# Cutting the side-row loads and running-row stores of two gather passes into fifths, one behind each group of steps

## What is computed

```
x = layernorm(x + EdgeConv(x, src, dst))            # max over a node's edges of MLP([x_i, x_j - x_i])
x = layernorm(x + NodeUpdate(x, mean of edge_attr))  # mean over the edges that leave a node
x = layernorm(x + Mean(x, src, dst))                 # msg = segment_sum(x[src], dst) / degree, gate, linear
x = layernorm(x + Attention(x, src, dst, types))     # segment softmax over dst of 4 heads, typed weights
```

## Time and profile before

| | |
|---|---|
| runs (us) | 19606.31, 19635.21, 19637.1; median 19635.21 |
| the profiled execution: its time, its span | 19425.3 us, 19423.5 us |
| POOL busy in the span | 13120.1 us, 68% |
| DVE busy | 7110.8 us, 37% |
| PE busy | 4712.7 us, 24% |
| SP's DMA queue (q1) | 1,029,704 packets, 830.45 MB, 14.2% of 16 DMA engines' span |
| POOL's DMA queue (q0) | 416,960 packets, 533.81 MB, 12.1% |

### The profile page before, as it was taken

The page is one execution under the profiler, slowest core; times in us unless marked ns, Lnnn a source line. Parts: engine busy times, 40 slices in busy tenths (PEclk is TensorE's granted clock), DMA queues, the critical chain, the costliest instruction groups (busy, mean ns, idle before and its releaser), DMA issues.

```text
span 19423.5 us, 125968 instructions
## 1 busy us (share of the span) xinstructions
PE 4712.7 (24%) x20806; PEld 3710.9 (19%) x20806; DVE 7110.8 (37%) x16320; ACT 1013.1 (5%) x4397; POOL 13120.1 (68%) x13050
## 2 busy tenths in 40 slices
PE   3221221221666666666510000000032000000002
PEld 2100010000566665566410000000021000000001
DVE  5444444443333433333331111111123444444444
ACT  0000000000000000000000000000022000000000
POOL 4666666667666666666657777777755666666665
PEclk9655555555555555555555555555566555555555
DMA  2222222221333333333211121211123333333332
GB/s 71 76 70 68 69 69 67 66 70 51 93 93 91 91 92 93 92 93 93 71 41 45 47 47 47 47 47 47 45 84 121 97 97 97 95 95 97 97 95 55
DMA packets 1464730, 1467.46 MB, mean 76 GB/s; under 512 B 727134, under 2 KB 1226293, under 8 KB 1464536
## 3 DMA queue, kind: packets, MB, share of 16 engines
q1 hardware_dynamic: 1029704, 830.45, 14.2%
q0 software_dynamic: 416960, 533.81, 12.1%
q10 hardware_dynamic: 18000, 102.41, 1.3%
HBM read 863.04 MB, written 602.69 MB: 75 GB/s over the span
## 4 chain that ended last, share of the span: by engine, by line
issue 31%; another core or an unknown queue 19%; DVE 18%; POOL 17%; PE 10%; DVEq 2%; DMA 2%; ACT 1%; SPq 0%; POOLq 0%; ACTq 0%
POOL gat L643 16%; PE pair L1011 4%; DVE oh_lo L1294 2%; DVE prod L1306 2%; DVE oh_hi L1296 2%; PE bank L1000 2%; DVE cur L1391 1%; DVE run_sb L1661 1%; DMA gat<-tab_t,gi 1%; DVE ar L1684 1%; DVE ag_idx L1310 1%; PE bank L1002 1%; PE bank L988 1%; DVE run_sb L1693 1%
## 5 line engine op out<-in xcount | busy, mean ns | idle before, releaser
L600 POOL DMA_INDIRECT perm<-at,ag_idx x3125 | 3135.3, 1003 | 1575.6 <-issue 937.5
L643 POOL DMA_INDIRECT gat<-tab_b,gi x3125 | 3121.2, 999 | 1588.0 <-issue 968.1
L643 POOL DMA_INDIRECT gat<-tab_x,gi x3125 | 3307.4, 1058 | 1191.1 <-issue 1187.7
L643 POOL DMA_INDIRECT gat<-tab_t,gi x3125 | 3027.8, 969 | 1373.5 <-issue 902.5
L1032 PE MATMUL pair<-ident,tails 128*64 128x128 f32 (+1 forms) x20 | 4.9, 421 | 8795.8 <-DVE tails L1474 4423.6
L1011 PE MATMUL pair<-blk,ohb 128*128 128x65 f32 x7500 | 1765.3, 422 | 12.5 <-DVE ohb L1416 12.3
L1032 PEld LDWEIGHTS pair<-ident,tails 128*64 128x64 f32 (+1 forms) x20 | 3.1, 170 | 8797.5 <-DVE tails L1474 4424.4
L1584 DVE TENSOR_TENSOR run_sb<-p,gat 128x320 f32<-128x320 f32 x625 | 314.9, 504 | 3702.2 <-DMA gat<-tab_x,gi 3691.9
L1011 PEld LDWEIGHTS pair<-blk,ohb 128*128 128x128 f32 x7500 | 1645.8, 329 | 88.0 <-DVE ohb L1416 14.0
L961 PE MATMUL bank<-oh_s,lo_bf 128*128 128x490 bf16 x625 | 368.2, 589 | 3219.1 <-DVE prod L1306 2638.4
L1290 DVE TENSOR_TENSOR oh_s<-iota_bf,st_sh 128x490 bf16<-128x490 bf16 x625 | 417.6, 668 | 1760.3 <-remote 1431.9
(11 more groups left out here) (283 smaller groups left out, 9830.6 us busy)
## 6 DMA issues: line engine op xcount, KB each, us to landing
edge<-start_rows SPq DMA_DIRECT2D x250, 800.0 KB
run<-run_sb SPq DMA_DIRECT2D x250, 800.0 KB
blk<-perm SPq DMA_DIRECT2D x750, 165.0 KB
run<-run_sb SPq DMA_DIRECT2D x125, 900.0 KB
at<-in_edge_attr SPq DMA_DIRECT2D x625, 160.0 KB
start_rows<-zeros ACTq DMA_DIRECT2D x125, 800.0 KB
tab_t<-trow SPq DMA_DIRECT2D x98, 512.0 KB
perm<-at,ag_idx POOLq DMA_INDIRECT x3125
```

Of the source, the lines that this page charges most:

```text
L600: pool.indirect_dma_start(perm_d, rows(perm_d, ag_idx[tp][:, k, s:s + 1]), at[tp][:, s, k, :], None).then_inc(a_sc[tp], 16)
L643: pool.indirect_dma_start(gat[:, k, s, 0:width], None, table, rows(table, gi[tp][:, s, k:k + 1])).then_inc(g_in[k], 16)
```

## The change

In passes c and d, SP issues each tile's store, and in pass d each tile's load, as five DMAs, one for each chain index s (a fifth: 128 pieces, one per partition; 160 KB, and 180 KB for the store of pass d). Fifth s waits for `t * KS + min(s, 3)` instead of `t * KS`, so the fifths come one behind each step of the tile, and the last two behind the same one. Loads and stores alternate. Pass b keeps its whole transfers. The waits of DVE at L1576, L1665 and L1666, of SP at the pass's end and of POOL before the node stages (L650) count five DMAs per tile in place of one. Nothing else changes.

```diff
             def edge_io(c, side_done, run_done, run_d, width, with_side):
+                in_fifths = c != "b"
...
+                def load_fifth(t, tp, s):
+                    sp.dma_start(edge0[tp][:, s].rearrange("p k f -> p (k f)"),
+                                 chains(starts_d)[:, s, bass.ds(t * (KS * F), KS * F)]).then_inc(e_in[tp], 16)
+
+                def store_fifth(t, tp, s):
+                    sp.dma_start(chains(run_d)[:, s, bass.ds(t * (KS * width), KS * width)],
+                                 run_view(tp, width)[:, s].rearrange("p k f -> p (k f)")).then_inc(r_out[tp], 16)
 
                 def body(t, tp):
...
-                    if with_side:
+                    if not in_fifths:
                         sp.wait_ge(side_done, t * KS)
                         load(t + 1, 1 - tp)
-                    sp.wait_ge(run_done, t * KS)
-                    store(t - 1, 1 - tp)
-
-                if with_side:
+                        sp.wait_ge(run_done, t * KS)
+                        store(t - 1, 1 - tp)
+                        return
+                    for s in range(SUB):
+                        step = min(s, KS - 2)
+                        if with_side:
+                            sp.wait_ge(side_done, t * KS + step)
+                            load_fifth(t + 1, 1 - tp, s)
+                        sp.wait_ge(run_done, t * KS + step)
+                        store_fifth(t - 1, 1 - tp, s)
...
+                if with_side and in_fifths:
+                    for tp in range(2):
+                        for s in range(SUB):
+                            load_fifth(tp, tp, s)
...
             def phase_d(t, tp, first):
                 v.wait_ge(d_st, t * 2 + 2)
-                v.wait_ge(e_in[tp], sides(1, t, tp))
-                v.wait_ge(r_out[tp], sides(2, t, tp))
+                v.wait_ge(e_in[tp], sides_d(t, tp))
+                v.wait_ge(r_out[tp], stored_by_fifths(2, t, tp))
```

34 lines of the change are left out of this document (24 added, 10 removed).

## The result

| | kernel before | changed kernel |
|---|---|---|
| runs | 13 | 13 |
| median (us) | 19615.96 | 19675.53 |
| lowest to highest (us) | 19592.66 to 19639.93 | 19635.13 to 19707.54 |
| ratio of the times | 1 | 1.0027, 95% interval 1.002 to 1.0034 |

What follows compares the result with a forecast made beforehand. POOL was taken to bound the kernel, busy 68% of the span. Terms -130 - 75 - 50 + 8 = -247 us took the profiled 19425.3 to 19178, or 19388 us for the runs' median; 8-in-10 range 18990 to 19720.

Steps and rivals of the forecast that it cites:

- The floor of 1.247 us a gather: POOL in passes c and d: 3125 gathers need 3897 us, leaving 459 and 504 us that smoother transfers could give back.
- The store in pass c, -130 us: Pass c: a whole store costs POOL 1.94 us, five fifths 0.85; 1.1 us gained in 118 tiles, 130 us.
- The price of a fifth, 0.85 us from pass b: Pass c: a tile's five fifths cost POOL 5 x 0.17 = 0.85 us, half of what pass b's block loads showed.
- The wait before the second step of pass d, -75 us: Pass d: the whole load delays gathers, so POOL waits 0.84 us; fifths save 0.6 us in 125 tiles, 75 us.
- The eighth of DVE's slow stretches, -50 us: Pass d: fewer slow DVE stretches coincide with late gathers, saving an eighth of the remaining 429 us, 50 us.
- SyncE's cost, taken as 0 with bounds 0 and 138 us: Pass d: SP issues ten DMAs a tile; DVE might wait 1.1 us for the last store, but 0 was taken.
- The ends, +8 us: Outside the loops of passes c and d: fifths add four issues of 0.64 us at three places, 8 us.
- Rival 1: Passes c and d: transfers were hidden anyway and stalls only move to other gathers; about 19606 us, chance 0.19.
- Rival 3: Pass d: SP falls behind issuing ten DMAs, so DVE waits for its last store; +250 us, 19885 us, chance 0.17.
- Rival 2: Passes c and d: transfer bursts make the slow stretches, so most surplus goes; 720 us less, 18915 us, chance 0.14.

Runs made afterwards that it cites:

- e2: Kernel before with stores in fifths in pass c only, pass d whole; 19593.07 us, ratio 0.9999.
- e5: Kernel before with each gather of pass c bringing rows to 64 partitions instead of 128; 19448.33 us, ratio 1.0003.
- e6: Kernel before with the stores of pass c holding 16 of 128 partitions; 19451.24 us, ratio 1.0005.
- e9: Kernel before with POOL gathering four of the five groups of a step in pass c; 18705.62 us, ratio 0.9536.
- e12: Kernel before with pass d's loads and stores moving 32 of 128 partitions, in whole transfers; 1.440 us a gather in the pass's middle.
- e3: Kernel before with loads and stores in fifths in pass d only, pass c whole; 19645.11 us, ratio 1.0029.
- e10: Kernel before with pass d's loads and stores in fifths, all ten behind a tile's first step; 19668.39 us, ratio 1.0027.
- e11: Kernel before with whole transfers and eight added one-row stores a tile in pass d; 19691.35 us, ratio 1.0036.
- e13: Kernel before with 24 more SyncE waits a tile in pass d (empty instructions absorbed), no further transfer; 19500.65 us, ratio 1.0037.
- e17: The changed kernel again, unaltered, on a chip without pauses; 16949.56 us, ratio 0.9974 to the kernel before.
- e14: Kernel before with whole transfers and sixteen added one-row stores a tile in pass d; 19521.74 us, ratio 1.0049.
- e15: Kernel before with 24 waits and 24 empty instructions a tile on TensorE in pass d; 17039.78 us, ratio 0.9999.
- e8: Kernel before with only pass d's loads in fifths, stores and pass c whole; 19478.95 us, ratio 1.0023.
- e16: Kernel before with 48 empty SyncE instructions a tile written into pass d, which left the program unchanged; 17040.1 us, ratio 1.0.
- e18: The kernel of e16 once more, in effect the kernel before; 16991.55 us, ratio 0.9999.
- e4: Kernel before with an empty POOL instruction ahead of each gather of pass c, which did not enter the program; ratio 0.9998.

## Why the prediction was wrong, step by step

**The floor of 1.247 us a gather was the step that failed.** I took the pace of the first 210 us of pass c for what POOL can do, and the 459 and 504 us above it for something that smoother transfers could give back. Where the pauses are, POOL gathers at 1.394 to 1.40 us in the long run, whatever stores and rows go with it (e2, e5, e6), and with a fifth fewer gathers the pass is a fifth shorter (e9). A pass c of 3125 gathers had a floor of some 4363 us, not 3897, and stood on it. What sets this pace is not shown. Whether it holds in pass d too isn't shown. There the gathers inside a step keep 1.27 us, and 3.5 of the 4.0 us a tile above 1.247 us a gather stand where POOL waits for DVE (before the change). The sum gave 125 us of that back to smoother transfers. With a quarter of their bytes the pass was no faster (e12).

**The store in pass c, -130 us.** Measured: nothing (e2, 0.9999), and 4 us without the pauses. The 1.94 us of the earlier trace rows stood behind a store, and I read them as caused by it. The place was right: the mean over the tiles has 1.91 us there. The cause was wrong: a store of an eighth of the bytes has 1.88 us there (e6). And the time isn't free to be had: it is part of what POOL's pace asks for, and lands in part on other gathers if the store is cut up (the timeline of the result). Rows that speak against it were in the argument: the early store of the earlier trace rows costs nothing, and I put that down to a steady state "that begins after the first 210 us" without asking what that state was. The price of a fifth, 0.85 us from pass b, has no counterpart either: the tile keeps its 35 us with one store or five.

**The wait before the second step of pass d, -75 us.** The mechanism was right. Without the pauses it gave 49 us, 0.67 us a tile instead of 0.6, less 0.28 that the fifths cost at other steps and for which the sum had no term. With the pauses it gave some 39 us, 0.31 us a tile (e3 against e2), and 94 us were lost at the other steps of the same tiles.

**The eighth of DVE's slow stretches, -50 us.** It went the other way. Those stretches are there only when the pauses are, and with more instructions of SyncE POOL's waits for DVE grew by 63 us in 4000 (e3 against e2).

**SyncE's cost, taken as 0 with bounds 0 and 138 us.** That it isn't 0 was within the bounds, for another reason than theirs. SyncE's transfers did come 4 to 5 us apart as the earlier trace rows had shown, but DVE hardly waited for the last store (7.4 us in 4000). What costs is SyncE's further instructions beside DVE's chain: 48 us with all at once (e10), 71 us with hardly any bytes (e11), 79 us with no further transfer (e13). Without the pauses no such cost shows at the starts of the steps, which stay at 1.25 us (e17). The sum priced the transfers and had no term for instructions.

**The ends, +8 us.** Nothing to see in the differences of the traces; too small to test.

**The rivals.** Rival 1, that the transfers were hidden anyway and the stall "only moves to other gathers" because of "a limit over a longer time", describes pass c, though with a tiny store the stall stayed where it was (e6). It had 0.19 and should have had most of the chance. Rival 3 had the sign and the place, SyncE, but its price was 250 us for 55, and its way through L1666 is refuted. Rival 2, slow stretches made by the bursts, is refuted by e6 and e12, where the bursts are an eighth and a quarter and the passes no shorter. The result lies inside the range, near its upper end, since of the 287 us between forecast and median 247 were the expected gain and 60 the loss, less 20 for the median of the kernel before, which came out at 19616 instead of 19635. That the range holds it is luck: its upper end was made up for rival 1 and a mild rival 3, and no term of the sum led there.

The Trainium skill's rule that each DMA engine alternates between queues packet by packet ("DMA: Bandwidth & Descriptors", section "Queues, rings and completion order") had been set aside because of the 3.2 us of the earlier trace rows. For pass c its consequence, no change, is what was measured (0.9999 in e2). For pass d it isn't: without the pauses the fifths took away 0.67 us at the step behind a whole load, and rows are used 4.23 us after the last gather where a whole load starts, so a whole load does hold gathers up.

**What stays open.** What the pauses are. No kernel here makes them come or go: they were in pass d of all traces up to e14 and of none from e15 on. The chip alone doesn't decide it: e5 to e8 (19446 us for the kernel before) and e15 and e16 (17040 us) bear the same chip number. Nor do the pages show more loading of code: the two queues marked `instruction` carry 66 packets in the kernel before with the pauses and 66 in e18 without. The Trainium skill ("NOTIFIC — the notification-queue block", section 7.1) says that the block's internal pipeline holds its producers back instead of losing a record. That would fit pauses of one length on two engines and a price by the number of instructions, but not that POOL and ACT show none. No run here varies it, so it is a guess. Open as well: what holds POOL at 1.394 us a gather in pass c, and why only after the first 170; whether waits and register instructions cost alike, whether those of another engine would cost the same (e15 met no pauses); and by what path SyncE's slow DVE's. The time of DVE's own slow instructions doesn't follow the loss: DVE's sequencer instructions sum to 385 us between 15000 and 19000 us in e2 and to 551 in e3, but to 341 in e8, which also lost 33 us.

No version beats both kernels everywhere. The changed one is the best without the pauses and the one before is with them. Fifths in pass d alone would be expected to do as well as the change in the first case (pass c gained 4 us); that wasn't run there.

## What to carry to other kernels

Before a surplus over an engine's best pace is booked as a gain, ask whether the pace is a limit over time: cut the number of the engine's instructions by a fifth and see whether the surplus goes with them, as e9 did. A stall that stands beside a transfer is no proof, neither in one tile nor in the mean. Average by position over all tiles, and look whether it shrinks when the transfer is made tiny. Here it didn't. And cutting a transfer in five isn't free on an engine with nothing to do: its instructions are on the chip beside those of the chain that sets the pace, and with two transfers a tile becoming ten it cost more here than it gave, as long as the pauses were about. The same mean by position shows both sides: what a change gives at its place and what it takes at the others.

## What the runs showed of the hardware that I had not expected

- In traces with pauses POOL's indirect gathers start 1.25 us apart for the first 150 to 170 of pass c and then some 1.40 us apart, with 128 rows or 64 (e5). In traces without pauses they keep 1.26 to 1.28 us through the pass (3932 us for 3125 in e18, 4000 in e16).
- Some register and semaphore instructions of SyncE and DVE take 0.70 us (medians 700 and 699 ns in e14) and a few 1.4, in pass d of all traces up to e14. In 4000 us of the kernel before they are 140 of SyncE's 736 and 306 of DVE's 5217. In pass d of those from e15 on they take under 0.04 us on average. POOL's and ACT's never take longer than 0.08 us there, and in pass c DVE's don't either. The kernel before took 19421 to 19620 us with them and 16993 to 17040 us without.
- SyncE needed 17.22 us to issue five transfers in a loop with the pauses. Five of the same loop in e17:

```profile
3020.44 4.38 SPq L446 DMA_DIRECT2D at<-in_edge_attr  x5
```

- Twenty-eight waits and register sums a tile, on an engine whose transfers nothing waited for, made the program 79 us longer (e13). That is 79 / (28 x 123) = 23 ns for each (13 to 29 by the interval).
- An empty instruction without a wait leaves no instruction behind (e4, e16, e18).
